# Macaron block with FP4 feed-forward on Trainium2: two neighbouring FFN tiles quantised as one

## What is computed

```python
x = x + 0.5 * ffn(layernorm(x))
x = x + attn(layernorm(x))
x = x + 0.5 * ffn(layernorm(x))

# attn, D = 256, no values' or output matrix
q = x @ Wq.T + bq;  k = x @ Wk.T + bk
a = softmax(q @ k.T / sqrt(D));  a = eye + a;  a = a - mean(a, -1)
return a @ x

# ffn: 704 hidden, every input and weight is quantised to FP4 in blocks of 16
def fp4_quant_dequant(x):
    scale = max(max(abs(xb)) / 6, 1e-12)        # per block of 16
    return GRID[searchsorted(MID, abs(xb / scale))] * sign(xb) * scale
def fp4_linear(x, w): return fp4_quant_dequant(x) @ fp4_quant_dequant(w).T
h = silu(fp4_linear(x, w_gate)) * fp4_linear(x, w_up)
return fp4_linear(h, w_down)
```

## Time and profile before

| | us |
|---|---|
| median of three runs | 2394.25 |
| the three runs | 2394.25, 2400.36, 2389.05 |
| the profiled execution, its own time | 2397.43 |
| its span in the profile | 2395.6 |

### The profile page before, as it was taken

One profiled execution on the slowest core, in us unless ns is written; L12 is line 12 of the kernel. 1 busy time (PEld: TensorE's weight loads), 2 busy tenths in 40 slices (PEclk: granted clock), 3 DMA queues, 4 the chain that ended last, 5 costly groups with the idle time before them and its releaser, 6 DMA issues. The chain is left out here.

```text
span 2395.6 us, 46422 instructions
## 1 busy us (share of the span) xinstructions
PE 2099.0 (88%) x13514; PEld 1249.1 (52%) x13514; DVE 2069.8 (86%) x3961; ACT 1674.6 (70%) x4315; POOL 750.7 (31%) x664
## 2 busy tenths in 40 slices
...
DMA packets 741596, 214.25 MB, mean 89 GB/s; under 512 B 706464, under 2 KB 741152, under 8 KB 741408
## 3 DMA queue, kind: packets, MB, share of 16 engines
...
## 5 line engine op out<-in xcount | busy, mean ns | idle before, releaser
L1163 PE MATMUL gu_ps<-wgu_hi,xT 128*128 128x512 f16 (+1 forms) x3072 | 956.9, 366 | 64.5 <-DMA xT<-f_dq 55.0
L586 POOL TENSOR_TENSOR tile_area<-tile_area,h_rs 128x704 f32<-128x704 f32 x256 | 390.3, 1525 | 1291.1 <-DVE h_rs L1076 1291.1
L1163 PE MATMUL gu_ps<-wgu_lo,xT 128*128 128x512 f16 (+1 forms) x1536 | 562.5, 366 | 0.0
L1163 PEld LDWEIGHTS gu_ps<-wgu_hi,xT 128*128 128x128 f16 x3072 | 303.6, 99 | 377.0 <-issue 63.2
L1264 PE MATMUL out_ps<-wd_hi,hT 128*128 128x256 f16 x1536 | 364.0, 280 | 134.8 <-DMA hT<-h_dq 134.8
L1264 PE MATMUL out_ps<-wd_lo,hT 128*128 128x256 f16 (+1 forms) x1536 | 378.4, 281 | 0.0
L959 DVE SCALAR_TENSOR_TENSOR tile_area<-gu_ps,gu_unit,tile_area 128x704 f32<-128x704 f32 x256 | 241.5, 944 | 130.1 <-PE gu_ps L1163 63.7
L851 ACT ACTIVATE tile_area<-gu_ps,gu_unit 128x704 f32<-128x704 f32 x256 | 215.5, 842 | 188.8 <-PE gu_ps L1163 188.4
L706 ACT ACTIVATE h_y<-tile_area 128x704 bf16<-128x704 f32 x256 | 200.3, 782 | 92.2 <-POOL tile_area L586 92.2
L1264 PEld LDWEIGHTS out_ps<-wd_hi,hT 128*128 128x128 f16 x1536 | 153.4, 100 | 203.0 <-issue 120.3
L971 DVE TENSOR_REDUCE h_am<-tile_area 128x44 f32<-128x704 f32 x256 | 227.1, 887 | 6.7
...
## 6 DMA issues: line engine op xcount, KB each, us to landing
...
hT<-h_dq SPq DMA_TRANSPOSE x256, 3.6
pT<-p SPq DMA_TRANSPOSE x128, 3.2
xT<-f_dq SPq DMA_TRANSPOSE x64, 4.3
...
```

What stands on the lines that cost most here:

```text
L586: g.tensor_tensor(blocks(h_xq[:, n % 2, :], FB), blocks(hid[:, n % 2, :], FB), per_block(h_rs[:, n % 2, 0:FB], FB), ALU.mult).then_inc(xq_ ...
L1163: ins = t_.matmul(dst, x, y, start=(i == 0), stop=(i == len(todo) - 1))
```

## The change

The change adds an item `duo`, which starts at every odd `j` and stands for two neighbouring tiles. Gate_up, silu, `hid`, `h_sh`, `h_sl`, the down product and the add stay per tile. The block maxima, their maxima, scales, reciprocals, the division on POOL, `h_unit`, `h_sigma`, `h_y`, t, q, dh and dl become one instruction for both tiles, over 1408 elements instead of 704 (over 90 instead of 45 for scales). On DVE 22 instructions for two tiles become 14, on ACT 10 become 7, on POOL 2 become 1; there are 128 duos.

`hid` gets a tensor of its own with four buffers, and the division writes in place. `h_t` and `h_q` have one buffer, `h_dq` two for a duo, `hT` four for single tiles. The folded weights lie in `qT` during the start. With this the order of every engine's list is written anew. On PE the three cuts of `gate_up` stand back to back, the two down products of a duo come one after the other ahead of the `gate_up` of every even slot, and the second half of `scores` of a query stands a slot after its first half, ahead of the downs. On POOL the first front's `f_ve`, `f_rstd` and `f_shift` come after all work on the weights. SP issues a duo's two transposes after `dl`.

```diff
-A_TURNS = (("q0", "afront", 3), ("q1", "afront", 3))
-OUT_TURNS = (("att0", "query", 5), ("att1", "query", 5), ("down", "tile", 3))
+A_TURNS = (("q0", "afront", 4), ("q1", "afront", 4))
+OUT_TURNS = (("down0", "duo", 5), ("down1", "duo", 5), ("att0", "query", 6), ("att1", "query", 6))
...
+            if "tile" in s.started and j % 2 == 1:
+                start(s, "duo")
...
-        tile_area = sb("tile_area", [P, 4, 2, FWRAP])
-        sg, hid, h_xq, h_t = (tile_area[:, i, :, 0:FF] for i in range(4))
-        h_y = sb("h_y", [P, 2, FF], BF16)
+        h_t = area[:, 0:2 * FF]
+        sg = area[:, 2 * FF:4 * FF].rearrange("p (i f) -> p i f", f=FF)
+        hid = sb("hid", [P, 4, FF])
+        hid2 = hid[:, :, :].rearrange("p (i e) f -> p i (e f)", e=2)
+        h_y = sb("h_y", [P, 2, 2 * FF], BF16)
...
-        h_dq = sb("h_dq", [P, 2, 2 * FF], F16)
-        hT = sb("hT", [P, 2, HC, P], F16)
+        h_dq = sb("h_dq", [P, 2, 2, 2 * FF], F16)
+        hT = sb("hT", [P, 4, HC, P], F16)
...
-                    g.tensor_tensor(blocks(h_xq[:, n % 2, :], FB), blocks(hid[:, n % 2, :], FB),
-                                    per_block(h_rs[:, n % 2, 0:FB], FB), ALU.mult).then_inc(xq_done.sem, 1)
+                    g.tensor_tensor(blocks(hid2[:, m % 2, :], 2 * FB), blocks(hid2[:, m % 2, :], 2 * FB),
+                                    per_block(h_rs[:, m % 2, 0:2 * FB], 2 * FB), ALU.mult).then_inc(xq_done.sem, 1)
...
-                    a_.activation(h_sh[:, n % 2, :, :], twice(h_s[:, n % 2, 0:FB], FB), ACT.Copy,
-                                  scale=h_unit[:, n % 2:n % 2 + 1]).then_inc(sh_done.sem, 1)
-                    a_.activation(h_y[:, n % 2, :], h_xq[:, n % 2, :], ACT.Abs, scale=LIFT).then_inc(lifted.sem, 1)
+                    a_.activation(h_sh[:, m % 2, 0:FB, :], twice(h_s[:, m % 2, 0:FB], FB), ACT.Copy,
+                                  scale=h_unit[:, m % 2, 0:1]).then_inc(sh_done.sem, 1)
+                    a_.activation(h_sh[:, m % 2, FB:2 * FB, :], twice(h_s[:, m % 2, FB:2 * FB], FB), ACT.Copy,
+                                  scale=h_unit[:, m % 2, 1:2]).then_inc(sh_done.sem, 1)
+                    a_.activation(h_y[:, m % 2, :], hid2[:, m % 2, :], ACT.Abs, scale=LIFT).then_inc(lifted.sem, 1)
...
+                    v.tensor_reduce(h_am[:, m % 2, 0:2 * FB], blocks(hid2[:, m % 2, :], 2 * FB), AX.X, ALU.max,
+                                    apply_absolute_value=True).then_inc(am_done.sem, 1)
+                    v.scalar_tensor_tensor(out=h_t[:, :], in0=h_y[:, m % 2, :], scalar=ROUND_MIN,
+                                           in1=hid2[:, m % 2, :], op0=ALU.max, op1=ALU.add).then_inc(t_done.sem, 1)
+                    v.scalar_tensor_tensor(out=h_q[:, :], in0=h_y[:, m % 2, :], scalar=ROUND_MIN,
+                                           in1=h_t[:, :], op0=ALU.max, op1=ALU.subtract).then_inc(q_done.sem, 1)
+                    v.tensor_tensor(duo_pairs(h_dq[:, m % 2, :, 0:FF]), duo_q(h_q[:, :]),
+                                    duo_scale(h_sh[:, m % 2, :, :]), ALU.mult).then_inc(dh_done.sem, 1)
+                    v.reciprocal(h_rs[:, m % 2, :], h_s[:, m % 2, :]).then_inc(rs_done.sem, 1)
...
+                if s.query[4] is not None:
+                    scores(half, 1).then_inc(score_full.sem, 1)
+                if s.duo[5] is not None:
+                    down(2 * m).then_inc(out_full.sem, 1)
+                    down(2 * m + 1).then_inc(out_full.sem, 1)
...
                     gate_up(n, 0).then_inc(gu_full.sem, 1)
...
                     gate_up(n, 1).then_inc(gu_full.sem, 1)
...
+                    gate_up(n, 2).then_inc(gu_full.sem, 1)
```

More of the change, by code:

```diff
@@ L88, in schedule @@
     slots = []
-    count = dict(tile=0, query=0, front=0, afront=0)
+    count = dict(tile=0, duo=0, query=0, front=0, afront=0)
     info = {"tile": [], "front": []}
@@ L119, in schedule @@
             past = slots[i - k].started
-            s.tile[k], s.query[k] = past.get("tile"), past.get("query")
+            s.tile[k], s.query[k], s.duo[k] = past.get("tile"), past.get("query"), past.get("duo")
             s.front[k], s.afront[k] = past.get("front"), past.get("afront")
@@ L126, in schedule @@
         for s in slots:
-            items = dict(tile=s.tile, query=s.query, front=s.front, afront=s.afront)
+            items = dict(tile=s.tile, duo=s.duo, query=s.query, front=s.front, afront=s.afront)
             for name, what, age in order:
@@ L820, in emit @@
+                    a_.activation(a_nm[:, 2:4], a_sum[:, 2:4], ACT.Copy, scale=-1.0 / D).then_inc(a_nm_done.sem, 1)
                 if s.afront[2] is not None:
@@ new lines, in emit @@
+                if s.duo[4] is not None:
+                    m = s.duo[4]
+                    ffn, seq, t = info["tile"][2 * m]
+                    src, dst = (x0, x1) if ffn == 1 else (x2, x3)
+                    dve.wait_ge(out_full.sem, out_full.at(turn_down[2 * m] + 1, pair))
+                    dve.wait_ge(sigma_done.sem, sigma_done.at(m + 1, pair))
+                    if ffn == 2 and t == 0 and (pair is not None or seq >= 2):
+                        dve.wait_ge(stored[seq % 2].sem, stored[seq % 2].at(16 * (seq // 2), pair))
+                    v.scalar_tensor_tensor(out=dst[:, seq % 2, t, :], in0=out_bank(turn_down[2 * m]),
+                                           scalar=h_sigma[:, m % 4, 0:1], in1=src[:, seq % 2, t, :],
+                                           op0=ALU.mult, op1=ALU.add).then_inc(out_added.sem, 1)
@@ new lines, in emit @@
+                if s.query[3] is not None:
+                    a = s.query[3]
+                    half = a % QPS
+                    dve.wait_ge(nmax_done.sem, nmax_done.at(a + 1, pair))
+                    dve.wait_ge(rho_done.sem, rho_done.at(a // QPS + 1, pair))
+                    v.scalar_tensor_tensor(out=s_mneg[:, :], in0=s_nmax[:, :], scalar=score_unit[:, :], in1=rho[:, 2 * half:2 * half + 2],
+                                           op0=ALU.mult, op1=ALU.subtract).then_inc(mneg_done.sem, 1)
@@ new lines, in emit @@
+                if s.duo[2] is not None:
+                    m = s.duo[2]
+                    dve.wait_ge(sh_done.sem, sh_done.at(2 * m + 1, pair))
+                    v.scalar_tensor_tensor(out=h_sl[:, m % 2, 0:FB, :], in0=twice(h_s[:, m % 2, 0:FB], FB),
+                                           scalar=h_unit[:, m % 2, 0:1], in1=h_sh[:, m % 2, 0:FB, :],
+                                           op0=ALU.mult, op1=ALU.subtract).then_inc(sl_done.sem, 1)
+                if s.query[6] is not None:
+                    a = s.query[6]
+                    seq, t = a // QPS, 2 * (a % QPS) + 0
+                    dve.wait_ge(out_full.sem, out_full.at(turn_att0[a] + 1, pair))
+                    v.scalar_tensor_tensor(out=x2[:, seq % 2, t, :], in0=out_bank(turn_att0[a]), scalar=1.0 / (SP * SX),
+                                           in1=x1[:, seq % 2, t, :], op0=ALU.mult, op1=ALU.add).then_inc(out_added.sem, 1)
```

916 lines of the change are left out of this document (453 added, 463 removed).

## The result

The changed kernel takes 2432.52 us (median of 4 runs, 2431.16 to 2433.21), the kernel before 2395.14 (4 runs, 2389.05 to 2400.36). The ratio is 1.0157, with a 95% interval of 1.0138 to 1.0176: 37 us slower, where 2439 us, 45 slower, were forecast. The span of the profiled execution is 2430.7 us, 35.1 more than before.

What follows compares the result with a forecast made beforehand. PE and DVE hold each other up, neither full. From 69.2 us a sequence, 1.2 less work and waits of 8.6 against 5.3 give 71.3, taken as 70.5: +36, start +2, end +7, so 2439 us; range 2366 to 2500.

Steps and rivals of the forecast that it cites:

- the sum: VectorE's waits over one sequence, places (a) to (f) added: 8.6 us against 5.3 before.
- (a): Step 5: s_nmax, directly behind both p_lo, waits for the scores; 2.2 us idle a sequence against 0.7 before.
- (b): Step 5: two downs stand behind the scores on PE, the second ending late for DVE; 0.9 us idle.
- (c): Step 1: ACT has xs_hi and h_unit, which waits for the reciprocal, ahead of hid's silu; 1.65 us idle.
- (d): Step 1: h_sl waits for h_sh behind four f_ss, or is held by POOL's xs_lo; 2.0 us, bounds 0 and 3.5.
- (e): f_am's wait on DVE, 0.6 us a sequence before, kept at 0.7.
- (f): Hardware loop turn, now falling on a dl with ACT and PE no further ahead; 1.2 us a sequence added.
- The case of dh and dl at one element a nanosecond: Rival C: the doubled products on DVE fall to a slower rate, 5.9 us a sequence, 2607 us; chance 0.03 with another rival.
- The rival that bigger instructions cost as two: Nothing saved on DVE by merging, +2.2 us more a sequence, 2500 us; chance 0.03 together with rival C.
- the walk: One sequence of the new order followed on paper with start-to-start durations and waits, without small gaps; ends at 70.2 us.
- Pace kept: Rival B: only PE and DVE hold each other, -0.9 us a sequence, 2378 us; needs (c) and (d) absent; chance 0.27.
- Even: Rival D: saving and new waits cancel, only the ends cost, 2403 us; chance 0.20.

Runs made afterwards that it cites:

- the later edits: Changed kernel with three order edits (step 5, ScalarE's step 1, loop turn): 2375.03 us; besides, both p_lo in step 4 and silu first in step 5: 2342.20 us.
- the second experiment: Changed kernel, only ScalarE's order in step 1: silu ahead of f_sum, xs_hi and h_unit; 2433.75 us.
- that edit: Changed kernel, only ScalarE: the four a_ss at the end of step 7, ahead of the loop turn; 2416.77 us.
- the split: Changed kernel with maxima, t, q and dh as two instructions of 704 elements each, dl one of 1408; 2443.10 us.
- the splits: Maxima, t, q and dh as two instructions each, dl whole: from the changed kernel 2443.10 us, from the three order edits together 2388.88 us.

## Why the prediction was right, and where it was not

**The engine and the direction.** It counted DVE's round, and said that work taken off DVE would be given back in waits at named places. The saving was larger than forecast (1.9 us a sequence by the windows, 1.2 forecast, bounds 0.6 and 2.2); which of its terms was too small no run tells. The waits came to 8.6, the number of the sum, and that is luck: the terms below miss in both directions. The first edit, which touches only the order of step 5, takes back all 37 us, and merging four of the eight kinds of instructions is worth 11 to 14 us in either order. So the loss is the new order's and not these bigger instructions'. No run takes back PE's new order, and none puts the later edits into the kernel before, so how much of the 51 us needs the merging isn't shown.

**Term by term.** (a) The scores: 2.2 forecast, 2.20 measured, and shown by the edit of step 5. (b) The second add: 0.9 and 0.94. (c) Silu in step 1: 1.65 forecast; measured 1.77 and 2.2 in turn, 2.0 in the mean. It didn't come from `h_unit` waiting for the reciprocal, which was there 0.7 early, but from `xs_hi` and what ran ahead of it on ACT. By itself it is worth nothing, as the second experiment shows; the sum treated it as additive. (d) `h_sl`: 2.0 forecast; measured 0.84 of wait and 0.38 of holding, 1.2. That was the term most oversized: the `h_sl` came so late that only the end of `xs_lo` held it. With ACT's order mended the holding was 1.87 in the rows shown. (e) `f_am` 0.7 and 0.54. (f) The turn: I wrote 1.2. DVE's own hole is 21.3/20 = 1.1, and behind it came 0.6 of silu wait that I had not seen as a matter of ACT, whose turn is twice as long; that edit gained 16 us. Two waits that the sum didn't have, at t and at dh, make 0.4 more. In waits alone (d) was 1.2 too high, and (c), (f) and these two made up for it.

**The sizes of instructions.** t and q 1.62 us (forecast near 1.6), dh 0.89 and dl 0.85 (near 0.9), the division 2.59 (near 2.6), the reciprocal 0.71 (0.7). The case of dh and dl at one element a nanosecond is out. That merging saves 0.07 us an instruction was nearly right as work (0.9 us for 16 instructions in the split, 0.06 each); the splits show that only a third to two thirds of it is time. The rival that bigger instructions cost as two is out as well, since DVE's work fell.

**PE.** Its wait for the hidden tile went down to 11.1 us, where none was forecast, and as forecast the wait for silu stands there instead (46.1 us). That the first moved nothing fits the time but was tested by no run.

**The sum.** Per sequence 70.28 against 70.5: +1.02 instead of +1.3. In spans: the first store comes 6.0 us later (forecast 2), the 28 sequences behind it add 25 (forecast 36), the drain adds 4.0 (forecast 7), 35 in all against 45. The start was the step that failed: the first gate_up begins at 72.6 us instead of 67.3, the 5 us that the prediction names, but the 3 us that should come back while the pipeline fills did not. Step 5 has a part in it: the first edit begins its gate_up at 72.9 and stores first at 302.9 us, 8.3 earlier than the changed kernel and 2.3 earlier than the kernel before. The forecast put the new order's waits into the 28 sequences alone, and the filling pipeline meets them too. How much each wait costs there is open. That 70.5 came so near to 70.28 rests partly on the choice to go down from 71.3 towards the walk.

**The rivals.** "Pace kept" needed (c) and (d) to be absent; they were there. "Even" failed for the changed kernel, but with one place mended gain and loss do cancel (2393).
